# A fused four-block network on one core: the fourth group's expert choice placed directly behind the third's in the first router, ahead of the second half of the second pair's projections

## The chip, the cores and the metric

The kernel runs on one core of one Trainium2 chip. The metric is device time in microseconds (us) of one execution of the whole program. The engines are TensorE (PE), VectorE (DVE), ScalarE (ACT), GpSimd (POOL) and SyncE (SP); each runs its own program in order, and they meet through semaphores.

## What is computed

Four blocks follow one another on x of shape (4, 1024, 256), each one normalised at its entry and added back: a gated recurrence, a mixture of 8 experts with two chosen for each token, causal attention with 16 heads, and a mixture of 32 experts with four chosen. The change lies where the first block ends and the router of the second begins:

```python
x = x + _L0_attn_ref(_layernorm(x), ...)        # ends with einsum('bsn,dn->bsd', h_seq, Wp) + bp
x = x + _L0_ffn_ref(_layernorm(x), w12, w3, gate_w)
# _L0_ffn_ref:
scores = jnp.einsum('btd,ed->bte', x, gate_w)
topk_scores, topk_idx = jax.lax.top_k(scores, 2)
topk_probs = jax.nn.softmax(topk_scores, axis=-1)
hidden = jax.nn.silu(h1) * h2                    # h12 = x @ w12 of the expert
y = jnp.sum(total_probs[..., None] * expert_out, axis=-2)
```

## The kernel before

The 4096 tokens are 32 tiles of 128 rows, kept in SBUF as `X`. The recurrence runs over two pairs of batches (p = 0 and 1), 16 tiles each, since one pair fills the 128 partitions with 2 times 64 states. Its last step is `projections(p, tiles)` on PE (one matmul for each tile) and `add_projections(p, tiles)` on DVE (the sum into `X`, and `bn_stats` of the tile before it); `pair_moments(p)` makes mean and inverse deviation of all 16 tiles of the pair.

The first router works on NG = 8 groups of 4 tiles, g = 0 to 7. Groups 0 to 3 (the first to the fourth) belong to the first pair of batches and groups 4 to 7 (the fifth to the eighth) to the second; GP is 4 and QT is 8. For one group the work goes from engine to engine:

- DVE `rows_of(g)`: the normalised rows into one of RBUF = 4 buffers `b_rows`. From group 4 on it needs `pair_moments(1)`.
- PE `router_transposes(g)`: 8 transposes into PSUM banks 6 and 7. ACT `take_xT(g)` copies them out. PE `router_scores(g)`: 16 small matmuls into bank 2 or 3.
- DVE `choose_pair(g)`: the two best of 8 scores, the score gap, the one-hot rows `b_ohs`. ACT `router_exp(g)`: the exponential of the gap. PE `count_before(g)`: how many tokens before each one went to the same expert.
- DVE `place_pair(g)`: gates and the row slots `b_slot`, from the counts. POOL then issues 8 indirect DMAs, which scatter the group's rows into the experts' regions of the DRAM tensor `routed0`.

`low_weights` and `high_weights` split the experts' first matrices in two parts for the tile products. They lie between the groups: ACT makes the high parts, DVE the low parts of the half k = 1 (eight calls) and six of the half k = 0, POOL the last two of k = 0. After group 7 a plan is made from the counts, the ends of the experts' regions are zeroed, and the loop over 71 expert tiles starts when the plan is there, all scatters have landed, and all low parts are ready.

All order on an engine is written out by hand. The scores and counts of group g share bank 2 + g % 2; `router_scores(g)` waits until the prefixes of group g - 2 have been read. SP has the stores of `X` and the zero fills of the accumulators in its own queue beside all this.

Of the kernel before, what the change touches and what calls it, by code (L numbers as in the profile page):

```python
# [45 lines left out]
def network(nc, x_in, a_params, w12T, w3T, gate0T, wqkT, wvT, woT, swT, bias1, ewT, out):  # L46
# [14 lines left out]
    NG = T // GT  # L61
# [6 lines left out]
    QT = S // P  # L68
# [17 lines left out]
    with ExitStack() as ctx:  # L86
# [370 lines left out]
        def tile_of(t, n):  # L457

            return X[:, bass.ds(t + n, 1), :].rearrange("p a d -> p (a d)")
# [145 lines left out]
        GP = 2 * S // GT  # L605
# [395 lines left out]
        def _(act):  # L1001
# [46 lines left out]
            def take_xT(g):  # L1048
                act.wait_ge(s_btp, g + 1)
                act.activation(b_xT[g % 2][:, :, :].rearrange("p k t -> p (k t)"),  # L1050
                               PS[:, 6:8, :].rearrange("p a n -> p (a n)"), ACT.Copy).then_inc(s_bxT, 1)

            def router_exp(g):

                act.wait_ge(s_bgap, g + 1)
                act.activation(b_ex[:, :], b_gap[:, :], ACT.Exp).then_inc(s_bex, 1)

            def high_weights(k, half):

                act.wait_ge(s_bw, 16 * E0 * KD)  # L1060
                for e in range(half * E0 // 2, (half + 1) * E0 // 2):
                    cols = slice(e * 2 * H0, (e + 1) * 2 * H0)
                    act.activation(b_w12h[k][:, cols], b_w12T[:, k, cols], ACT.Copy).then_inc(s_wh, 1)
# [29 lines left out]
            scan_exps(1, 2)  # L1093
            take_xT(1)
            for g in range(1, NG):
                if g + 1 < NG:
                    take_xT(g + 1)
                router_exp(g)
                if g in (GP - 1, GP):
                    high_weights(1, g + 1 - GP)  # L1100
                if g == NG - 2:

                    act.wait_ge(s_bxn, NT)
                    act.wait_ge(s_xs, 16 * (NG + 1))
                if g >= NG - 2:
                    high_weights(0, g + 2 - NG)
# [369 lines left out]
        def _(dve):  # L1476
# [62 lines left out]
            def add_projections(p, tiles):  # L1539

                for n in tiles:
                    dve.wait_ge(s_abp, p * (2 * QT) + (n + 1))
                    dve.wait_ge(s_ay, p * (2 * QT) + (n + 1))
                    dve.tensor_tensor(tile_of(p * (2 * QT), n), PS[:, 4 + n % 2, 0:D], tile_of(p * (2 * QT), n),
                                      ALU.add).then_inc(s_x1, 1)

                    if n:
                        dve.wait_ge(s_x1, p * (2 * QT) + n)
                        st.done(dve.bn_stats(a_stat[:, n - 1, :], tile_of(p * (2 * QT), n - 1)))
# [14 lines left out]
            def rows_of(g):  # L1564

                if g >= RBUF:
                    dve.wait_ge(s_bxnf, g - RBUF + 1)
                apply_norm(dve, g * G, b_rows[g % RBUF][:, :, 0:D], s_bxn)
# [31 lines left out]
            def place_pair(g):  # L1600

                n = g % RBUF
                st.done(dve.tensor_reduce(b_gsum[:, :], b_ohs[:, :, :].rearrange("p g e -> p e g"), AX_X, ALU.add))

                dve.wait_ge(s_bex, g + 1)
                st.done(dve.tensor_scalar(b_den[:, :], b_ex[:, :], 1.0, None, ALU.add))
                st.sync()
                st.done(dve.reciprocal(b_den[:, :], b_den[:, :]))
                st.sync()
                st.done(dve.tensor_tensor(b_rows[n][:, :, SECOND], b_den[:, :], b_ex[:, :], ALU.mult))  # L1610
                st.sync()
                st.done(dve.tensor_tensor(b_rows[n][:, :, GAP], b_den[:, :], b_rows[n][:, :, SECOND], ALU.subtract))
                dve.wait_ge(s_bpre, g + 1)
                pre = PS[:, 2 + g % 2, 256:256 + G * E0].rearrange("p (g e) -> p g e", g=G)
                for k in range(K0):
                    st.done(dve.tensor_tensor(b_tmp[:, :, k, :], b_oh[:, :, k, :], pre, ALU.mult))
                st.sync()
                dve.sem_inc(s_bpr, 1)
                st.done(dve.tensor_tensor(b_sum[:, :], b_sum[:, :], b_gsum[:, :], ALU.add))
                st.done(dve.tensor_reduce(b_pos[:, :, :].rearrange("p g k -> p (g k)"),  # L1620
                                          b_tmp[:, :, :, :].rearrange("p g k e -> p (g k) e"), AX_X, ALU.add))
                st.sync()
                st.done(dve.scalar_tensor_tensor(b_slot[n][:, :, :], idx, float(REGION), b_pos[:, :, :], ALU.mult, ALU.add))
                st.sync()
                dve.sem_inc(s_bslot, 1)
# [20 lines left out]
            add_projections(1, range(QT))  # L1646
            choose_pair(2)
            place_pair(2)
            add_projections(1, range(QT, 2 * QT))
            pair_moments(1)  # L1650
            rows_of(4)
            for g in range(GP - 1, NG):
                choose_pair(g)
                if g >= GP:
                    low_weights(1, 2 * (g - GP) + 1)
                place_pair(g)
                if g < NG - 1:
                    low_weights(1, 2 * (g + 1 - GP))
                if g + 2 < NG:
                    rows_of(g + 2)  # L1660
# [466 lines left out]
            for n in range(2):  # L2127
                g = NG - 2 + n
# [75 lines left out]
        def _(pe):  # L2204
# [28 lines left out]
            def projections(p, tiles):  # L2233

                pe.wait_ge(s_ah, p + 1)
                for n in tiles:
                    b, t = n // QT, n % QT
                    if n >= 2 or p:

                        pe.wait_ge(s_x1, p * (2 * QT) + (n - 1))  # L2240
                    else:
                        pe.wait_ge(s_axT, GP * KD)
                    pe.matmul(PS[:, 4 + n % 2, 0:D], a_h[p][:, t * P:(t + 1) * P], a_wpT[b], start=True, stop=True).then_inc(s_ay, 1)
# [21 lines left out]
            def count_before(g):  # L2265

                pe.wait_ge(s_boh, g + 1)
                for q in range(G):
                    dst = PS[:, 2 + g % 2, 256 + q * E0:256 + (q + 1) * E0]
                    pe.matmul(dst, onesb[:, :], b_sum[:, :], start=True, stop=False)  # L2270
                    for r in range(q):
                        pe.matmul(dst, onesb[:, :], b_ohs[:, r, :], start=False, stop=False)
                    ins = pe.matmul(dst, tri[:, :], b_ohs[:, q, :], start=False, stop=True)
                ins.then_inc(s_bpre, 1)
# [16 lines left out]
            router_transposes(1)  # L2291
            router_scores(1)
            for g in range(1, NG):
                if g + 1 < NG:
                    router_transposes(g + 1)
                count_before(g)
                if g + 1 < NG:
                    router_scores(g + 1)
                if g <= 2:
                    projections(1, range((g - 1) * QT, g * QT))  # L2300
            pe.wait_ge(s_boh, NG + 1)
            pe.matmul(PS[:, 0, 0:E0], onesb[:, :], b_sum[:, :], start=True, stop=True).then_inc(s_bpre, 1)
            pe.wait_ge(s_bplan, 2)
# [605 lines left out]
```

## Time and profile before

| | |
|---|---|
| median of 3 runs | 2199.08 us (2198.98 to 2201.33) |
| the profiled execution, its own time | 2198.34 us |
| its span in the profile | 2196.1 us |
| mean granted PE clock | 0.935 of full speed |

The profile is of one execution. Times in it are microseconds from the start of the span. A row of a timeline has the start, the length, the engine, the line, the operation and the tiles out<-in; the number in square brackets is the idle time of that engine before the row, and what ended it. "remote" is a release that the profile can't put down to an instruction, and "issue" is time in which it shows no wait. Line numbers are those of the code above.

### The profile page before, as it was taken

How to read it: one execution, taken by the hardware profiler on the slowest of the kernel's cores; microseconds unless marked ns; L12 is line 12 of the kernel's file. 1: busy time of each engine (PE TensorE's matmuls, PEld its weight loads, DVE VectorE, ACT ScalarE, POOL GpSimd, SP SyncE). 2: the span in 40 equal slices, each digit the busy share in tenths (PEclk: the TensorE clock that was granted, in tenths of full speed). 3: DMA queues.
4: the chain of work that ended last, by engine and by line, in shares of the span. 5: the costliest groups of instructions: out<-in, count | busy, mean ns of one | idle time of the engine just before them, and what ended most of it. 6: DMA issues, size and time to landing. Idle time of an engine off the chain costs nothing. (4 is left out here: it accounts for less than half of the span.)

```text
span 2196.1 us, 42575 instructions
## 1 busy us (share of the span) xinstructions
PE 1923.5 (88%) x11815; PEld 1444.0 (66%) x11816; DVE 1361.8 (62%) x3638; ACT 1079.2 (49%) x2250; POOL 1175.1 (54%) x1159
## 2 busy tenths in 40 slices
PE   4852999999689999999999999999999999974870
PEld 2541788888567677677777677777677777752660
DVE  6765343443367777656777656777656877653763
ACT  5321334333355555646655546555646565521760
POOL 3455233232216665536587735577845677835782
PEclk8765999999889999999999999999999999986995
DMA  9652533333331211211121101121101121121979
GB/s 337 213 204 83 125 51 51 51 51 53 79 91 50 56 51 48 54 32 53 50 75 44 48 24 53 50 57 48 45 28 52 47 59 46 39 94 53 205 132 255
DMA packets 215710, 177.59 MB, mean 81 GB/s; under 512 B 85442, under 2 KB 200727, under 8 KB 214880
## 3 DMA queue, kind: packets, MB, share of 16 engines
q1 hardware_dynamic: 177904, 138.78, 21.5%
q0 software_dynamic: 28656, 27.61, 8.3%
q10 hardware_dynamic: 8960, 8.92, 1.2%
q8 instruction: 88, 1.44, 0.3%
q14 instruction: 102, 0.84, 0.1%
HBM read 95.05 MB, written 80.72 MB: 80 GB/s over the span
## 5 line engine op out<-in xcount | busy, mean ns | idle before, releaser
L950 POOL TENSOR_TENSOR c_den_late<-c_den_late,c_p 128x512 f32<-128x512 f32 (+3 forms) x384 | 408.9, 1065 | 247.6 <-ACT c_p L1259 203.6
L1259 ACT ACTIVATE c_p<-PS 128x512 f32<-128x512 f32 (+3 forms) x768 | 342.9, 491 | 230.1 <-PE PS L2470 128.6
L2491 PE MATMUL PS<-c_p,c_vh 128*64 128x256 f32 (+1 forms) x2816 | 322.0, 349 | 0.0
L2439 PE MATMUL PS<-c_k,c_q 128*128 128x512 f32 (+2 forms) x768 | 288.2, 376 | 16.3 <-DVE c_max L1828 5.2
L2462 PE MATMUL PS<-c_q,c_k 128*128 128x512 f32 (+2 forms) x768 | 287.4, 378 | 4.1 <-issue 1.8
L2491 PEld LDWEIGHTS PS<-c_p,c_vh 128*64 128x64 f32 x2816 | 204.5, 137 | 102.5 <-issue 39.7
L886 POOL DMA_INDIRECT acc<-b_y,b_tok x71 | 110.5, 1557 | 277.6 <-ACT b_y L1129 242.9
L2463 PE MATMUL PS<-c_q,c_k 128*128 128x512 f32 (+2 forms) x768 | 258.9, 348 | 0.0
L1250 ACT ACTIVATE c_q<-PS 64x512 fp32r<-64x512 f32 x256 | 151.3, 591 | 205.3 <-PE PS L2426 178.4
L1835 DVE CUSTOM_DVE_ANT_0 PS<-PS,c_maskq,c_max 128x128 f32<-128x128 f32 (+3 forms) x256 | 143.0, 559 | 126.1 <-PE PS L2439 90.8
L1828 DVE TENSOR_REDUCE c_max<-PS 128x1 f32<-128x512 f32 x256 | 175.0, 684 | 55.1 <-PE PS L2439 52.5
L950 POOL TENSOR_TENSOR c_den<-c_den,c_p 128x384 f32<-128x384 f32 (+2 forms) x192 | 141.3, 736 | 120.1 <-ACT c_p L1259 94.8
L2439 PEld LDWEIGHTS PS<-c_k,c_q 128*128 128x128 f32 x768 | 145.6, 190 | 89.4 <-DVE c_max L1835 29.2
L1835 DVE CUSTOM_DVE_ANT_0 PS<-PS,c_maskq 128x128 f32<-128x128 f32 (+3 forms) x256 | 125.9, 501 | 113.8 <-PE PS L2439 101.8
L2462 PEld LDWEIGHTS PS<-c_q,c_k 128*128 128x128 f32 x768 | 145.0, 189 | 33.1 <-issue 15.8
L919 POOL DMA_INDIRECT routed<-r_rows,r_slot x128 | 129.3, 1010 | 61.4 <-DVEq L1946 33.6
L1716 DVE SCALAR_TENSOR_TENSOR b_hid<-b_sg,PS 128x512 f32<-128x512 f32 x71 | 48.8, 688 | 177.4 <-issue 129.6
L2463 PEld LDWEIGHTS PS<-c_q,c_k 128*128 128x128 f32 x768 | 145.3, 189 | 8.8
L2347 PE MATMUL PS<-b_w3T,b_hT 128*128 x568 | 134.7, 380 | 2.0 <-ACT b_hT L1120 1.1
L2330 PE MATMUL PS<-b_w12h,b_tT_hi 128*128 x284 | 129.0, 454 | 5.5 <-DVE b_tT_lo L1709 5.5
L2518 PE MATMUL PS<-c_wo,c_yT 128*128 128x256 f32 x512 | 124.6, 387 | 0.0
L990 POOL DMA_INDIRECT acc<-d_y,d_tok x64 | 100.2, 1566 | 40.7 <-ACT d_y L1439 22.6
(304 smaller groups left out, 4008.8 us busy)
## 6 DMA issues: line engine op xcount, KB each, us to landing
c_vh<-c_v SPq DMA_DIRECT2D x64, 256.0 KB
c_rrow<-rden SPq DMA_DIRECT2D x63, 256.0 KB, 3.7
routed<-b_empty SPq DMA_DIRECT2D x32, 289.0 KB, 9.5
d_xe<-routed SPq DMA_DIRECT2D x32, 289.0 KB
b_xt<-routed SPq DMA_DIRECT2D x71, 130.0 KB
b_w12T<-in_w12T_dram SPq DMA_DIRECT2D x16, 512.0 KB, 13.3
d_acc<-acc SPq DMA_DIRECT2D x16, 512.0 KB, 8.7
c_st_hi<-wqk_split SPq DMA_DIRECT2D x48, 128.0 KB
```

The costliest lines, as they stand in the source:

```text
L919: pool.indirect_dma_start(routed1, bass.IndirectOffsetOnAxis(ap=r_slot[n][:, j // K1, j % K1:j % K1 + 1], axis=0), r_rows[n][:, j // K1, : ...
L950: pool.tensor_tensor(den[:, off:], den[:, off:], p, ALU.add).then_inc(s_cPa, 1)
L1250: act.activation(dst, src, ACT.Copy).then_inc(s_cqs, 1)
L1259: act.activation(c_p[:, P_AT[h][m]:P_AT[h][m] + WIDTH[m]], PS[:, ST_BANK[m % STB], skip:skip + WIDTH[m]], ACT.Exp, scale=ATT_SCALE).then_i ...
L1828: dve.tensor_reduce(dst, src, AX_X, ALU.max).then_inc(s_turn[bank], 1)
L1835: dve.tensor_tensor_reduce(src, src, c_maskq[:, 512 - w:512], 1.0, dst if c else BIG, ALU.add, ALU.max, dst).then_inc(s_turn[bank], 1)
L2330: pe.matmul(PS[:, 2 * j + c, :], b_tT[0][:, j, k, :], b_w12h[k][:, cols], start=(k == 0), stop=False)
L2347: ins = pe.matmul(PS[:, 6 + j, 0:D], b_hT[:, j, k, :], b_w3T[:, k, bass.ds(e * D, D)], start=(k == 0), stop=(k == KH - 1))
L2439: pe.matmul(PS[:, 2 + use[0], 0:max(w, 256)], c_q1[h][:, t * P:(t + 1) * P], c_k1[h][:, c * 512:c * 512 + max(w, 256)], start=True, stop=T ...
L2462: pe.matmul(PS[:, bank, 0:n], c_k1[h][:, j * P:(j + 1) * P], c_q1[h][:, q], start=True, stop=False)
L2463: ins = pe.matmul(PS[:, bank, 0:n], c_k2[h][:, j * P:(j + 1) * P], c_q2[h][:, q], start=False, stop=not diagonal)
L2491: ins = pe.matmul(dst, c_vh[h][:, j, :], moving, start=(j == 0), stop=(t0 == 2 + a))
```

## The change

Three programs are reordered; no instruction is added or removed. The choice and the slots of group 3 move on DVE from behind `pair_moments(1)` and `rows_of(4)` to directly behind group 2's; on PE the count of group 3 moves ahead of the second half of the projections and of the transposes of group 4, and the second half of the projections moves behind that count; on ACT the copy of group 4's transposed rows moves behind the exponential of group 3. On DVE `low_weights(1, 0)` and `rows_of(5)`, which stood around group 3's slots, now follow `rows_of(4)` in the other order.

```diff
@@ scalar engine
             for g in range(1, NG):
-                if g + 1 < NG:
+                if g + 1 < NG and g != GP - 1:
                     take_xT(g + 1)
                 router_exp(g)
+                if g == GP - 1:
+                    take_xT(g + 1)
                 if g in (GP - 1, GP):
                     high_weights(1, g + 1 - GP)
@@ vector engine
             add_projections(1, range(QT))
             choose_pair(2)
             place_pair(2)
+            choose_pair(GP - 1)
+            place_pair(GP - 1)
             add_projections(1, range(QT, 2 * QT))
             pair_moments(1)
-            rows_of(4)
-            for g in range(GP - 1, NG):
+            rows_of(GP)
+            rows_of(GP + 1)
+            low_weights(1, 0)
+            for g in range(GP, NG):
                 choose_pair(g)
                 if g >= GP:
                     low_weights(1, 2 * (g - GP) + 1)
@@ tensor engine
             for g in range(1, NG):
+                if g == GP - 1:
+                    count_before(g)
+                    projections(1, range(QT, 2 * QT))
                 if g + 1 < NG:
                     router_transposes(g + 1)
-                count_before(g)
+                if g != GP - 1:
+                    count_before(g)
                 if g + 1 < NG:
                     router_scores(g + 1)
-                if g <= 2:
-                    projections(1, range((g - 1) * QT, g * QT))
+                if g == 1:
+                    projections(1, range(QT))
```

## Rows read from the trace of the kernel before

**Rows 1.** the page: the span, and busy us, share and instructions of each engine

```profile
span 2196.1 us, 42575 instructions
...
PE 1923.5 (88%) x11815; PEld 1444.0 (66%) x11816; DVE 1361.8 (62%) x3638; ACT 1079.2 (49%) x2250; POOL 1175.1 (54%) x1159
```

**Rows 2.** timeline of DVE (start, us, engine, line, operation; idle before in brackets)

```profile
117.62 0.28 DVE L1616 TENSOR_TENSOR b_tmp<-b_oh,PS 128x32 f32<-128x32 f32 x2
...
118.38 0.17 DVE L1623 SCALAR_TENSOR_TENSOR b_slot<-b_idx,b_pos 128x8 uint32<-128x8 f32 x1
121.89 0.42 DVE L1544 TENSOR_TENSOR X<-PS,X 128x256 f32<-128x256 f32 x1 [3.34 <-issue]
...
128.20 0.41 DVE L1554 BATCH_NORM_STATS2 a_stat<-X 128x6 f32<-128x256 f32 x1
```

**Rows 3.** timeline of PE: scores, projections, transposes, counts

```profile
117.16 3.56 PE L2261 MATMUL PS<-b_gwT,b_xT 128*128 128x8 f32 x16
120.57 0.77 PE L2243 MATMUL PS<-a_par,a_li 128*128 128x256 f32 x1
...
134.67 1.97 PE L506 MATMUL PS<-ident,b_rows 128*128 128x128 f32 x8 [7.83 <-DVE b_rows L499]
136.94 0.19 PE L2270 MATMUL PS<-b_sum,onesb 128*128 128x8 bf16 x1 [0.30 <-DVEq L1598]
...
137.75 3.58 PE L2261 MATMUL PS<-b_gwT,b_xT 128*128 128x8 f32 x16 [0.28 <-ACT b_xT L1050]
...
144.92 0.19 PE L2270 MATMUL PS<-b_sum,onesb 128*128 128x8 bf16 x1 [0.43 <-issue]
```

**Rows 4.** timeline of DVE, from the fifth group's norm to its choice

```profile
133.23 1.38 DVE L499 TENSOR_SCALAR b_rows<-X,means,rstds 128x256 f32<-128x256 f32 x4
134.53 0.18 DVE L1576 COPY b_s<-PS 128x32 f32<-128x32 f32 x1
...
141.09 1.38 DVE L499 TENSOR_SCALAR b_rows<-X,means,rstds 128x256 f32<-128x256 f32 x4
142.38 0.18 DVE L1576 COPY b_s<-PS 128x32 f32<-128x32 f32 x1
```

**Rows 5.** timeline of ACT, the first high part of the weights

```profile
137.69 1.05 ACT L1063 ACTIVATE b_w12h<-b_w12T 128x1024 fp32r<-128x1024 f32 x1
```

**Rows 6.** timeline of DVE, its long idle times from 145 to 177

```profile
151.28 0.28 DVE L1616 TENSOR_TENSOR b_tmp<-b_oh,PS 128x32 f32<-128x32 f32 x2 [4.29 <-remote]
...
166.14 0.19 DVE L1576 COPY b_s<-PS 128x32 f32<-128x32 f32 x1 [3.27 <-remote]
...
172.98 0.17 DVE L1606 TENSOR_SCALAR b_den<-b_ex 128x4 f32<-128x4 f32 x1 [2.50 <-issue]
...
176.26 0.29 DVE L1616 TENSOR_TENSOR b_tmp<-b_oh,PS 128x32 f32<-128x32 f32 x2 [2.50 <-remote]
```

**Rows 7.** busy us of each engine by stretch, PE clock, DMA share, GB/s

```profile
145.00:150.00 5.00, 4.03 (x30) 3.85 (x30) 1.88 (x6) 4.42 (x6) 3.76 (x4) 0.50 0.95 312
150.00:155.00 5.00, 0.08 (x1) 0.08 (x2) 3.36 (x11) 0.00 (x0) 2.16 (x2) 0.50 0.09 32
```

**Rows 8.** timeline of POOL, scatters of the groups and the first low part

```profile
127.77 0.97 POOL L867 DMA_INDIRECT routed<-b_rows,b_slot  x1 [0.30 <-issue]
...
152.54 1.88 POOL L867 DMA_INDIRECT routed<-b_rows,b_slot  x1 [2.87 <-DVEq L1625]
...
177.53 1.88 POOL L867 DMA_INDIRECT routed<-b_rows,b_slot  x1 [3.63 <-DVEq L1625]
...
198.56 2.36 POOL L860 TENSOR_TENSOR b_w12l<-b_w12T,b_w12h 128x1024 fp32r<-128x1024 f32 x1
```

**Rows 9.** timeline of DVE, then of PE, before the first tile

```profile
199.65 3.65 DVE L1700 TENSOR_TENSOR b_tt<-b_tt,b_ts 128x71 f32<-128x71 f32 x1 [1.68 <-remote]
...
211.80 0.79 PE L2330 MATMUL PS<-b_w12h,b_tT_hi 128*128 x1 [4.24 <-DVE b_tT_lo L1709]
```

**Rows 10.** timeline of DVE beside the second router's last scatters

```profile
2001.75 0.69 DVE L2117 SCALAR_TENSOR_TENSOR d_sh<-d_sth,PS 128x512 f32<-128x512 f32 x1 [8.50 <-issue]
```

## The prediction

> **What bounds the kernel now.** I read the page first. PE is busy for 1923.5 of 2196.1 us, DVE, ACT and POOL for about half of it [rows 1], so over the whole kernel PE is the bound. The change lies in a stretch of some 95 us in which this isn't so, and only what moves the end of that stretch, the start of the first expert tile on PE at 211.80 us [rows 9], can move the total: the tile loop, the attention and the last block run behind it in the same order with the same work, so a shift of that start should pass through one to one.
>
> Next I read the timelines of this stretch, engine by engine. DVE ends the slots of the third group at 118.55 (118.38 + 0.17) and then idles for 3.34 us until the first sum of the second half of the projections at 121.89 [rows 2], which PE could begin only at 120.57, behind the fourth group's scores (117.16 + 3.56) [rows 3]. The sums and the moments are a chain of DVE and PE. After them DVE normalises the fifth group at 133.23, and between that and the choice of the fifth group's experts at 142.38 it does the fourth group's choice and slots, one low part, and the sixth group's norm [rows 4]. PE was idle for 7.83 us before the fifth group's transposes [rows 3]. Behind 142.38 come four groups of the same pattern, with POOL's scatters behind them.
>
> Third, I looked for what ends the stretch. POOL starts the fifth group's scatters at 152.54 and the seventh's at 177.53, each time after idling for DVE's slots (2.87 and 3.63 us) [rows 8]. So here POOL follows DVE and not the reverse. Its first low part starts at 198.56 [rows 8], and one of the plan's last operations on DVE, from 199.65 on, takes 3.65 us, until POOL is through with its two low parts [rows 9]. The chain that counts is DVE's, from 121.89 by way of 142.38 to the last slots and the plan.
>
> The fourth thing to see is four idle times of DVE between 145 and 177: 4.29, 3.27, 2.50 and 2.50 us [rows 6], together 12.56. The first is a wait for the fifth group's counts. PE began these at 144.92 [rows 3] and they are short, but DVE went on only at 151.28. The release came more than 5 us late. While it was pending the DMA engines had a share of 0.95, and in the next 5 us 0.09 [rows 7]. I call these late releases.
>
> **The change, step by step.** Nothing is added, so all is in when each piece runs.
>
> Step 1, the choice of the fourth group in the old gap. It can start when its scores are there, 120.72. From its start to the first count matmul the same choice took 136.94 - 134.53 = 2.41 us [rows 3, 4], so PE counts from 123.13. The count lasts no longer than 137.75 - 136.94 = 0.81, of which 0.28 is idle time before the scores, so 0.53 [rows 3]: it ends at 123.66, and only then can PE project. Before, it did at 120.57. The projections, sums and moments, and so the fifth group's norm, shift by 123.66 - 120.57 = **+3.09 us**: the first sum from 121.89 to 124.98, the norm from 133.23 to 136.32. DVE's slots of the fourth group cost nothing extra: from the counts on they took 118.55 - 117.62 = 0.93 [rows 2], so they end at 124.59, 0.4 us ahead of that first sum; the cover is thin, and any lateness of the counts adds to the 3.09.
>
> Step 2, the stretch behind the norm. Before, DVE's own work was its length: 142.38 - 133.23 = 9.15 us. With the fourth group gone it has the two norms and one low part, and the chain through the other engines becomes the length: norm until the transposes 134.67 - 133.23 = 1.44, transposes and ACT's copy until the scores 137.75 - 134.67 = 3.08, scores 3.58, together 8.10 us [rows 3, 4]. The choice of the fifth group begins at 136.32 + 8.10 = 144.42 instead of 142.38: **+2.04 us**. DVE's low part waits for ACT's first high part, which takes 1.05 [rows 5] and starts behind the copy; DVE waits for it in the time that PE has the scores, so it costs nothing; with the cover gone it would cost a little over 1 us.
>
> Step 3, POOL. The fourth group's scatters, whose slots came behind the fifth's norm in the old order, now go directly behind the third's last one, which ends at 128.74 (127.77 + 0.97). A group's eight take (177.53 - 152.54 - 3.63) / 2 = 10.7 us [rows 8], so they are through near 139.5, and POOL is free long before the fifth group's slots. It was waiting for those before too, so the earlier scatters by themselves give nothing. They do leave the DMA queues while SP stores `X` and the fifth group's counts are pending.
>
> Step 4, the late release of 4.29 us. In the new order the fifth group's counts begin 144.92 - 142.38 = 2.54 us behind its choice as before, near 147.0; no scatter is in flight, and the stores share the engines with nothing else, so that they should be finished sooner than at 150. Both things that stood beside the late release are gone. No row tells its cause. From both sides: it stays whole (0) or goes whole (-4.29). I take **-4.29**, since the nearest row on the other side, the busy DMA stretch, is the one that changes.
>
> Step 5, the three later idle times, 8.27 us together. They lie beside the last four groups' scatters, whose order isn't changed. Bounds: all gone (-8.27), or one more of the size seen beside the second router's last scatters, 8.50 us [rows 10]. I take 0.
>
> Sum: +2.04 - 4.29 = -2.25 us. DVE's chain and the scatters behind it shift together, and so does the first tile. The profiled execution took 2198.34 us (its span and 2.24 around it), which gives 2196.1; it was 0.74 below the median of the runs, so against the median of 2199.08 the forecast is 2196.8 us.
>
> At the end of the stretch a rule of the Trainium skill can be held against a row. The 3.65 us operation has both inputs in SBUF and ends at 203.30, POOL's two low parts at 198.56 + 2 x 2.36 = 203.28 [rows 8, 9]. SBUF — State Buffer, "Who interferes with whom", says that such a DVE operation contends with a GpSimd one that reads SBUF, and that the shared port pair is held for the whole instruction; the trace agrees. By the row alone I count nothing here, as both engines shift together. By the rule, a DVE that came 1.1 us earlier relative to POOL would get through first.
>
> **The rivals.**
>
> Rival 1, the late release stays. If 151.28 was fixed by the end of SP's stores, which come no earlier, the later counts are absorbed and the sum is 0: 2199.1 us. If it stays as a length, +2.04: 2201.1. For it: SP's stores are a queue of their own, and the share of 0.95 [rows 7] is mostly theirs. Against it: the scatters' share of the bytes is gone.
>
> Rival 2, slower. Third and fourth groups' scatters now run without a gap from just behind the slots of 118.55 to about 139.5, across the whole second half of the projections. DVE waits there for PE eight times, and every release that is late moves the norm. Beside long runs of scatters releases came late by 3.27 [rows 6] and by 8.50 us [rows 10]. At 8.50 the sum is +6.25: 2205.3. It ends beyond 0.2% only if the lateness exceeds 4.4 + 2.25 = 6.65 us. For it: the run is as long as those. Against it: beside the third group's scatters, in the old order, the sums from 121.89 to 128.61 kept their pace [rows 2].
>
> Rival 3, clearly faster. The three later idle times go too, in whole: 2.04 - 12.56 = -10.52, 2188.6 us. For it: no order of work demands them. Against it: the scatters beside them are unchanged.
>
> Rival 4, DVE gets ahead of POOL at the end and saves what the 3.65 us operation waited, at most about 3.4: -5.65, 2193.4 us. For it: only 1.09 us (199.65 - 198.56) of lead are missing. Against it: POOL was waiting for DVE too, so both shift alike. This is the case in which the skill's rule above would show.
>
> **How the numbers follow.** 0.2% of 2199 is 4.4 us; less than that a measurement of this kernel can't tell from no change. Forecast 0.44, rival 1 0.10, rival 2 0.18, rival 3 0.17, rival 4 0.11. Forecast and rival 1 are the same within 0.2%: 0.54. Faster: 0.28. Slower: 0.18. The range takes in the bounds of the late releases on both sides, 2188.6 to 2205.3, rounded to 2189 and 2205; the forecast's own range is 2194 to 2201. What is sure in the sum is small and against the change; what could be large is the releases, in either direction.
>
> **What the profile after would show.** Step 1: the first sum of the second half near 125.0, the fifth group's norm near 136.3. Step 2: its choice near 144.4, with DVE idle before it. Step 3: no gap between the third and fourth groups' scatters, and POOL idle from 139.5 to 150. Step 4: the fifth group's slots no later than 150, or else the idle time before them still ends at 151. Step 5: idle times of about 8 us between 150 and 175, the first tile on PE near 209.5. The prediction is wrong if releases come late among the projections, or if the idle times of the last four groups differ by more than 4 us from 8.27.

## The result and the profile after

| | before | after |
|---|---|---|
| median | 2197.61 us (14 executions, 2194.01 to 2201.33) | 2205.80 us (14 executions, 2201.52 to 2209.92) |
| the profiled execution, its own time | 2198.34 us | 2207.58 us |
| start of the first expert tile on PE | 211.80 us | 221.07 us |

The ratio is 1.0038 with a 95% interval of 1.0030 to 1.0046: the change makes the kernel slower by 8.2 us. The forecast was 2196.8 us, and the range ended at 2205. Between the two profiled executions lie 9.24 us, and the first tile starts 9.27 us later, so the whole loss arises ahead of it, and I read only that stretch.

The page, the span and the busy times: nothing has become more work (before in [rows 1]).

```profile
span 2205.5 us, 42575 instructions
...
PE 1925.8 (87%) x11815; PEld 1445.5 (66%) x11816; DVE 1364.3 (62%) x3638; ACT 1078.5 (49%) x2250; POOL 1175.2 (53%) x1159
```

The timeline of DVE, from the third group's slots to the fifth group's, answers to [rows 2, 4]. L1618 is the read of the counts, L1625 the slots, L1546 the sum of a projection into `X`, L499 the norm, L1578 the start of a choice.

```profile
118.73 0.17 DVE L1625 SCALAR_TENSOR_TENSOR b_slot<-b_idx,b_pos 128x8 uint32<-128x8 f32 x1
...
129.26 0.28 DVE L1618 TENSOR_TENSOR b_tmp<-b_oh,PS 128x32 f32<-128x32 f32 x2 [4.12 <-remote]
...
130.78 0.42 DVE L1546 TENSOR_TENSOR X<-PS,X 128x256 f32<-128x256 f32 x1 [0.59 <-remote]
...
132.23 0.42 DVE L1546 TENSOR_TENSOR X<-PS,X 128x256 f32<-128x256 f32 x1 [0.69 <-remote]
...
133.66 0.42 DVE L1546 TENSOR_TENSOR X<-PS,X 128x256 f32<-128x256 f32 x1 [0.68 <-PE PS L2249]
...
137.94 0.42 DVE L1546 TENSOR_TENSOR X<-PS,X 128x256 f32<-128x256 f32 x1 [2.07 <-PE PS L2249]
...
142.24 0.42 DVE L1546 TENSOR_TENSOR X<-PS,X 128x256 f32<-128x256 f32 x1 [2.09 <-PE PS L2249]
...
148.01 2.67 DVE L499 TENSOR_SCALAR b_rows<-X,means,rstds 128x256 f32<-128x256 f32 x8
...
156.14 0.19 DVE L1578 COPY b_s<-PS 128x32 f32<-128x32 f32 x1 [1.47 <-PE PS L2267]
...
160.54 0.28 DVE L1618 TENSOR_TENSOR b_tmp<-b_oh,PS 128x32 f32<-128x32 f32 x2
...
161.29 0.17 DVE L1625 SCALAR_TENSOR_TENSOR b_slot<-b_idx,b_pos 128x8 uint32<-128x8 f32 x1
```

Two things catch the eye. The read of the fourth group's counts stands behind 4.12 us of idle time, and seven of the eight sums behind some more, up to 2.09. And at 160.54 the read of the fifth group's counts has no idle time at all, where it had 4.29 before [rows 6].

The timeline of PE, counts and projections (before in [rows 3]):

```profile
123.83 0.19 PE L2276 MATMUL PS<-b_sum,onesb 128*128 128x8 bf16 x1 [2.77 <-DVEq L1600]
...
124.22 2.05 PE L2249 MATMUL PS<-a_par,a_li 128*128 128x256 f32 x4
131.26 1.22 PE L2249 MATMUL PS<-a_par,a_li 128*128 128x256 f32 x2 [4.98 <-issue]
...
138.42 1.22 PE L2249 MATMUL PS<-a_par,a_li 128*128 128x256 f32 x2 [1.61 <-issue]
```

PE has done the counts by 124.4, but DVE reads them at 129.26, 4.9 us later. Then PE itself waits for DVE's first sum (130.78) and goes on at 131.26: from here the two engines take turns, and from sum to sum it is mostly 1.45 or 2.85 us (130.78 to 132.23, 139.39 to 142.24), where the kernel before needed 0.65 to 1.2.

The timeline of POOL, the last scatter of the third group, the first and last of the fourth, and the first of the fifth:

```profile
128.13 0.97 POOL L867 DMA_INDIRECT routed<-b_rows,b_slot  x1 [0.30 <-issue]
130.52 0.96 POOL L867 DMA_INDIRECT routed<-b_rows,b_slot  x1 [1.42 <-issue]
...
139.43 0.97 POOL L867 DMA_INDIRECT routed<-b_rows,b_slot  x1 [0.31 <-issue]
161.79 1.88 POOL L867 DMA_INDIRECT routed<-b_rows,b_slot  x1 [21.39 <-DVEq L1627]
```

The sixteen scatters cover 119.2 to 140.4 with a gap of 1.42 us, and all late turns lie within or just behind them. DVE's idle times behind the fifth group (before in [rows 6]), from its timeline:

```profile
175.41 0.19 DVE L1578 COPY b_s<-PS 128x32 f32<-128x32 f32 x1 [3.28 <-remote]
...
183.70 0.17 DVE L1608 TENSOR_SCALAR b_den<-b_ex 128x4 f32<-128x4 f32 x1 [3.74 <-issue]
...
185.54 0.28 DVE L1618 TENSOR_TENSOR b_tmp<-b_oh,PS 128x32 f32<-128x32 f32 x2 [1.06 <-remote]
```

The balance, in starts of DVE's operations:

| stretch | before | after | difference | forecast |
|---|---|---|---|---|
| up to the fifth group's norm | 133.23 | 148.01 | +14.78 | +3.09 |
| norm to the fifth group's choice | 9.15 | 8.13 | -1.02 | -1.05 |
| choice to the fifth group's slots | 9.66 | 5.15 | -4.51 | -4.29 |
| slots to the first tile on PE | 59.76 | 59.78 | +0.02 | 0 |
| sum | | | +9.27 | -2.25 |

Three of the four terms came out within 0.25 us. The whole miss is in the first.

### The profile page after: what moved, and what is told of

It reads as the page before. It is cut to its first block and busy times, and to the rows that moved or that the text cites. A ratio compares the mean times of both kernels' runs of the same rounds, so it can differ in the third digit from the quotient of the medians.

```text
span 2205.5 us, 42575 instructions
## 1 busy us (share of the span) xinstructions
PE 1925.8 (87%) x11815; PEld 1445.5 (66%) x11816; DVE 1364.3 (62%) x3638; ACT 1078.5 (49%) x2250; POOL 1175.2 (53%) x1159
## 5 line engine op out<-in xcount | busy, mean ns | idle before, releaser
L2528 PE MATMUL PS<-c_wo,c_yT 128*128 128x256 f32 x512 | 124.4, 387 | 0.0
```

## Experiments

Kernels that ran together stand in one set, on the same chip and against the same runs of the kernel before. The median of the kernel before differed from set to set: 2193.23, 2178.59, 2179.65, 2180.04 and 2194.89 us in sets 1 to 5. This turned out to be part of the answer.

The theories. A: releases come late while scatters are in flight; the change puts the counts' release and the turns of PE and DVE under two groups' scatters. B: only the wait for the counts costs, because the slots of the fourth group, now ahead of the first sum, hold up everything behind them. C: SP's zero fills, not the scatters, make releases late.

**Set 1, undo or hold one thing at a time.** First the placing of the fourth group behind the norm, as before, with its choice and counts left where the change has them:

```diff
             choose_pair(GP - 1)
-            place_pair(GP - 1)
             add_projections(1, range(QT, 2 * QT))
             pair_moments(1)
             rows_of(GP)
+            place_pair(GP - 1)
```

> The changed kernel, but DVE makes the fourth group's slots (place_pair(3)) only behind the fifth group's norm; its choice stays ahead of the second half of the sums, and the order of PE and ACT is that of the change. In the changed kernel DVE idled 4.12 us for the fourth group's counts ahead of the first sum, and the first sum came at 130.78 us. Theory A (the second half of the projections is slow because the fourth group's scatters run beside it, and DVE waits for counts whose release comes late): here both are gone. The first sum comes near 125, the sums take about 7 us instead of 13.2, the fifth group's norm comes near 137 instead of 148.0, and the total is 6 to 9 us below the changed kernel. Theory B (only the wait for the counts in front of the sums costs): the first sum near 125.5, but the sums as slow as in the change, the norm near 143, 4 to 5 us gained. Theory C (the zero fills that SP issues in this stretch are what makes releases late, whatever POOL does): the sums keep their 13 us and their two idle times of 2 us, under 5 us gained.

Measured: 2200.70 us, ratio 1.0026 (1.0010 to 1.0041). From the timelines of DVE and of PE:

```profile
128.93 0.42 DVE L1546 TENSOR_TENSOR X<-PS,X 128x256 f32<-128x256 f32 x1 [6.59 <-remote]
...
135.20 0.42 DVE L1546 TENSOR_TENSOR X<-PS,X 128x256 f32<-128x256 f32 x1
```

```profile
122.85 2.05 PE L2249 MATMUL PS<-a_par,a_li 128*128 128x256 f32 x4
129.41 2.08 PE L2249 MATMUL PS<-a_par,a_li 128*128 128x256 f32 x4 [4.50 <-issue]
```

B falls: with no slots in the way the first sum is nearly as late, 6.1 us behind the start of its projection, and the sums, once begun, keep their pace; here the fourth group's scatters start only at 143.7. The two losses are separate. None of the three expectations for this kernel came in whole: A had the first sum near 125 and the norm near 137, and they came at 128.93 and 140.32; the third group's scatters (from 118.17) still stood beside the first projections.

Next, the order of the change with the fourth group's scatters held until all sums are done, and then with both groups' held (`g == 2` in place of 3):

```diff
                 pool.wait_ge(s_bslot, g + 1)
+                if g == 3:
+                    pool.wait_ge(s_x1, 2 * GP * G)
+                    pool.sem_inc(s_pass, 1)
```

> The changed kernel, but POOL begins the fourth group's scatters only when all sums of the second pair are made (one more wait on POOL). DVE still makes the slots ahead of the sums. Theory A (scatters in flight make PE's releases late): the 4 us wait for the counts near 125 stays, since the third group's scatters are in flight there, and the first sum comes near 130 again; from then on no scatter is in flight, so the sums take 6 to 7 us instead of 13.2 and the norm comes near 142 instead of 148.0; the total is 4 to 6 us below the changed kernel, if the fourth group's scatters then don't delay the fifth group's counts. Theory C (the zero fills do it): nothing changes up to the norm, total within 2 us of the changed kernel.

> The changed kernel, but POOL begins the third group's scatters only when all sums of the second pair are made, and so the fourth group's behind them. From 118.9 us until the last sum no scatter is in flight; SP's zero fills are. Theory A: the wait for the fourth group's counts is short (under 1 us), the first sum comes near 125 and the last near 131; the fifth group's norm near 137 instead of 148.0. The sixth group's norm then waits for the third group's scatters (they free its buffer), which costs some 10 us behind that, so the total tells little and the place of the norm decides. Theory C (zero fills): the wait for the counts stays near 4 us and the norm stays near 148.

Measured: 2197.74 us, ratio 1.0017 (1.0005 to 1.0030), and 2197.44 us, ratio 1.0020 (1.0009 to 1.0031). From the timeline of DVE with both held:

```profile
118.47 0.17 DVE L1628 SCALAR_TENSOR_TENSOR b_slot<-b_idx,b_pos 128x8 uint32<-128x8 f32 x1
...
125.24 0.42 DVE L1549 TENSOR_TENSOR X<-PS,X 128x256 f32<-128x256 f32 x1 [0.22 <-DVE b_slot L1628]
...
136.37 2.69 DVE L499 TENSOR_SCALAR b_rows<-X,means,rstds 128x256 f32<-128x256 f32 x8
...
153.27 0.17 DVE L1611 TENSOR_SCALAR b_den<-b_ex 128x4 f32<-128x4 f32 x1 [3.70 <-issue]
```

Without scatters in flight the first sum comes at 125.24 and the norm at 136.37; the forecast had 124.98 and 136.32. So the order of work costs what Step 1 said, and the rest is lateness. With only the fourth group's held, DVE still waits 3.73 us for the counts and the norm is at 140.28, but the sums run at their pace. With both held, the scatters then run across the fifth group's choice, where DVE now waits 3.70 us: the lateness has moved, and neither version beats the kernel before. Both profiles are of the fastest execution of their kernel (2192.78 and 2192.53 us, some 5 below the medians), so their places weigh more than their totals.

Last, the change with SP's zero fills behind the stores of `X`:

```diff
+            sp.dma_start(acc0[T:T + P, :], zeros[:, :]).then_inc(s_xs, 16)
+            for g in range(GP, NG):
+                store_x1(g)
             with sp.Fori(0, NT + C1 // P) as r:
                 sp.dma_start(acc[1][...], zeros[:, :]).then_inc(s_dax, 16)
             ...
-            sp.dma_start(acc0[T:T + P, :], zeros[:, :]).then_inc(s_xs, 16)
-            for g in range(GP, NG):
-                store_x1(g)
```

> The changed kernel, but SP issues the 36 zero fills of the second router's accumulators behind the stores of X instead of in front of them, so that from some 100 us until the last sum the DMA engines carry the scatters alone. Theory A (scatters make releases late): the wait for the fourth group's counts and the slow sums stay, the norm stays within 2 us of 148.0 us, total within 3 us of the changed kernel, unless the fills now meet the last groups. Theory C (zero fills make releases late, alone or together with the scatters): the wait for the counts falls under 1 us and the sums take 6 to 7 us, the norm comes near 137, and the total is 6 to 11 us below the changed kernel.

Measured: 2203.01 us, ratio 1.0039 (1.0026 to 1.0052). From the timeline of DVE:

```profile
124.37 0.28 DVE L1618 TENSOR_TENSOR b_tmp<-b_oh,PS 128x32 f32<-128x32 f32 x2 [1.11 <-PE PS L2279]
...
134.35 0.42 DVE L1546 TENSOR_TENSOR X<-PS,X 128x256 f32<-128x256 f32 x1 [2.04 <-PE PS L2249]
```

C holds for the counts (1.11 us of waiting in place of 4.12) and fails for the sums, which stay slow. In this profile fills and scatters together make the first wait; the scatters alone suffice for the second. The norm is 3.9 us earlier than in the change (144.12), but DVE later waits 4.56 us for the sixth group's counts, and the total gains nothing.

**Set 2, the same questions from the side of the kernel before.** The kernel before and the change once more, the kernel before with the fills moved as above, and the change with this edit on POOL:

```diff
+                if g == GP - 2:
+                    pool.wait_ge(s_bslot, GP)
+                    pool.sem_inc(s_pass, 1)
```

> The kernel before, unchanged, profiled a second time, to see how far a late release belongs to the order of the work and not to one execution. If late releases follow from which transfers are in flight when an engine releases another, the sums of the second half again keep their pace (first near 121.9 us, fifth group's norm near 133), and the idle time in front of the fifth group's slots is again 3 to 5 us. If they are chance, these differ by several us. Ratio to the kernel before 1.000.

> The changed kernel, unchanged, profiled a second time on the chip of this job. If the late releases belong to the order of the work: 3.5 to 5 us of idle time for the fourth group's counts near 125, slow sums, the norm between 145 and 150 us, ratio 1.0038 again. If they are chance: a norm anywhere from 136 to 150.

> The kernel before, but with SP's 36 zero fills behind the stores of X. In the changed kernel the same edit took the wait for the fourth group's counts from 4.1 to 1.1 us, left the sums slow, and gave nothing in total (1.0039 against 1.0038). Theory A (long runs of scatters make releases late): the sums were prompt before and stay so, norm near 133; the fifth group's counts still meet the fourth group's scatters, so that idle time stays at 3 us or more; total within 3 us of the kernel before. Theory C (the fills): that idle time falls under 1 us, and the total is 3 to 5 us below the kernel before, unless the fills, which now meet the last four groups, take it back.

> The changed kernel, but POOL begins the third group's scatters only when the fourth group's slots are made, so both groups' 16 scatters run from about 125 to 146 us. Theory A: no scatter is in flight when PE releases the fourth group's counts, so DVE waits for them under 1 us and the first sum comes near 125.2, as where both were held. The sums then run beside the first 7 us of a run of scatters. If releases come late only some 6 to 9 us into a run, the sums take 6 to 8 us and the norm comes at 136 to 139 instead of 148.0, and what comes late is the transposes and scores of the fifth group. If they come late at once, the norm comes at 141 or later. Total between 1.001 and 1.003 of the kernel before.

Measured, against a kernel before of 2178.59 us: 2178.20 (ratio 0.9993, 0.9984 to 1.0003), 2179.40 (1.0006, 0.9994 to 1.0018), 2178.76 (0.9995) and 2182.27 us (1.0011, 0.9998 to 1.0023). The expectations that counted on late releases missed, and the set doesn't answer what I had asked: no release came late in any of its kernels. The change, timeline of DVE and then of POOL:

```profile
115.24 0.17 DVE L1625 SCALAR_TENSOR_TENSOR b_slot<-b_idx,b_pos 128x8 uint32<-128x8 f32 x1
...
121.70 0.42 DVE L1546 TENSOR_TENSOR X<-PS,X 128x256 f32<-128x256 f32 x1 [0.22 <-DVE b_slot L1625]
...
132.17 2.81 DVE L499 TENSOR_SCALAR b_rows<-X,means,rstds 128x256 f32<-128x256 f32 x8
```

```profile
146.09 1.88 POOL L867 DMA_INDIRECT routed<-b_rows,b_slot  x1 [10.26 <-DVEq L1627]
...
190.51 4.64 POOL L860 TENSOR_TENSOR b_w12l<-b_w12T,b_w12h 128x1024 fp32r<-128x1024 f32 x2
```

The norm is 16.93 us behind the third group's slots, against 13.59 in the kernel before: +3.34, where Step 1 had +3.09. The first tile starts only 0.49 us later (197.15 against 196.66), or 1.16 us counted from the third group's slots (81.91 against 80.75), since POOL goes without a gap from 146.09 to its low parts at 190.51 (190.07 before) and is the bound here, not DVE. So without lateness the change costs about 1 us, 0.05%. The kernel before, too, has its first tile 15.1 us earlier here than in the profile that the prediction was made from (196.66 against 211.80), none of which is owed to the code. Its four idle times of [rows 6] are gone too.

**Sets 3 and 4, the same on two more chips.** Kernel before, change, and the two kernels with held scatters; in set 4 without the one that holds the fourth group's alone.

> The kernel before, a third profile, on the chip on which the next three run. Two kinds of chip have shown so far: one on which releases come late (kernel before at 2193 to 2199 us) and one on which none does (2178 us, fifth group's norm at 129.5 us, no idle time of DVE over 1 us up to the plan). On the first kind: norm near 133, first tile on PE near 212. On the second: first tile near 197. Ratio 1.000.

> The changed kernel beside it. On a chip with late releases: ratio 1.003 to 1.005, norm 12 to 15 us behind that of the kernel before. On one without: ratio 1.000 to 1.001, norm 2.7 us behind, first tile 0.5 us behind.

> The changed kernel with the fourth group's scatters held until the last sum, now on the same chip as the change. On a chip with late releases: wait for the counts still 3 to 5 us, sums prompt, norm 6 to 8 us ahead of the change, 3 to 6 us less in total. On one without: norm as in the change, and the total the same or up to 2 us above it, since POOL, which is then the bound, starts later.

> The changed kernel with the third and the fourth group's scatters held until the last sum, on the same chip as the change. On a chip with late releases: no wait for the counts, norm 11 to 12 us ahead of the change and 3 us behind the kernel before; total 3 to 6 us below the change. On one without: norm as in the change, but POOL's scatters of six groups then run without a gap from the last sum near 127 us on, so the first tile comes 4 us later than in the change or more, ratio 1.002 to 1.004.

> The kernel before, on the chip of this job. Norm of the fifth group near 133 us, with idle times of DVE of 2 to 5 us behind it, if releases come late on this chip; near 129.5 us and none if they don't.

> The changed kernel, on the same chip. If releases come late here: ratio 1.003 to 1.005, norm 12 to 15 us behind that of the kernel before. If not: ratio 1.000 to 1.001, norm 3 to 4 us behind.

> The changed kernel with the third and fourth groups' scatters held until the last sum, on the same chip. If releases come late here: norm 3 us behind the kernel before and 9 to 12 us ahead of the change, total 3 to 6 us below the change; that would show on one chip that the scatters in flight are the condition. If not: ratio 1.002, as on the last chip.

Measured: no late releases in either. The kernel before, run again, stands at 1.0003 (0.9991 to 1.0015) and 0.9990 (0.9978 to 1.0003), the change at 1.0002 (0.9991 to 1.0013) and 1.0005 (0.9992 to 1.0018), the fourth group's scatters held at 1.0006 (0.9996 to 1.0016), both groups' held at 1.0018 (1.0007 to 1.0028) and 1.0016 (1.0003 to 1.0029). Where there is nothing to save by holding scatters, holding them only starts POOL later: counted from the third group's slots, with both held in set 3, its low parts begin after 78.20 us instead of 75.24 in the change, and the first tile after 84.77 instead of 82.01.

**Set 5, the three kernels that matter on one chip.**

> The kernel before, on the chip of this job. With late releases on this chip: norm of the fifth group near 133 us, and idle times of DVE of 2 to 5 us behind it. Without: norm near 129.5.

> The changed kernel, on the same chip. With late releases: ratio 1.003 to 1.005, norm 12 to 15 us behind the kernel before. Without: ratio 1.000 to 1.001, norm 3 to 4 us behind.

> The changed kernel with the fourth group's scatters held until the last sum, on the same chip. With late releases: norm 6 to 8 us ahead of the change, total 3 to 6 us less. Without: the same as the change within 0.1%.

Here the lateness was back. Measured: 2196.40 us (ratio 1.0005, 0.9992 to 1.0017), 2204.38 us (four executions; 1.0048, 1.0031 to 1.0065) and 2198.40 us (1.0025, 1.0011 to 1.0039). From the timelines of DVE, the kernel before, then the change, then the change with the fourth group's scatters held:

```profile
134.37 1.38 DVE L499 TENSOR_SCALAR b_rows<-X,means,rstds 128x256 f32<-128x256 f32 x4
...
152.38 0.28 DVE L1616 TENSOR_TENSOR b_tmp<-b_oh,PS 128x32 f32<-128x32 f32 x2 [4.26 <-remote]
```

```profile
130.54 0.29 DVE L1618 TENSOR_TENSOR b_tmp<-b_oh,PS 128x32 f32<-128x32 f32 x2 [4.66 <-remote]
...
148.72 2.67 DVE L499 TENSOR_SCALAR b_rows<-X,means,rstds 128x256 f32<-128x256 f32 x8
```

```profile
129.03 0.28 DVE L1621 TENSOR_TENSOR b_tmp<-b_oh,PS 128x32 f32<-128x32 f32 x2 [4.14 <-remote]
...
142.20 2.69 DVE L499 TENSOR_SCALAR b_rows<-X,means,rstds 128x256 f32<-128x256 f32 x8
```

The late releases stand where they stood in the result's own profiles, with similar lengths (4.26 and 4.29, 4.66 and 4.12). One held scatter group takes 6.5 us off the norm, 5.0 of them behind the third group's slots (28.71 - 23.72 in the table below), and 6.0 us off the median.

All runs with lateness, and one without for each kernel, in one table. The columns count from the start of the third group's slots, so that what came ahead drops out; the last column is the first tile on PE.

| kernel (set) | to the first sum | first sum to last statistics | to the fifth group's norm | first tile |
|---|---|---|---|---|
| before (the result's) | 3.51 | 6.31 | 14.85 | 211.80 |
| before (5) | 3.12 | 5.92 | 14.85 | 213.00 |
| change (the result's) | 12.05 | 12.79 | 29.28 | 221.07 |
| change (5) | 12.07 | 12.19 | 28.71 | 221.52 |
| slots behind the norm (1) | 11.26 | 6.95 | 22.65 | 216.23 |
| fourth held (1) | 11.24 | 6.46 | 22.39 | 211.25 |
| fourth held (5) | 12.08 | 6.95 | 23.72 | 215.36 |
| fills moved (1) | 7.29 | 12.27 | 25.86 | 219.09 |
| both held (1) | 6.77 | 6.44 | 17.90 | 212.77 |
| before (2), none late | 3.08 | 6.06 | 13.59 | 196.66 |
| change (2), none late | 6.46 | 6.03 | 16.93 | 197.15 |

The first column separates the third group's scatters and the fills, the second the fourth group's scatters.

**Is it PE's clock?** PE's granted clock stood at 0.50 (1.2 GHz, the lower of its two levels) through the change's sums, while in the kernel before it rose to 1.00 (2.4 GHz) among them. That doesn't explain the turns. In set 5, with the fourth group's scatters held, PE had the same clock, shown here by stretch (PE, PEld, DVE, ACT, POOL, then clock, DMA share, GB/s), and the sums took 6.95 us instead of 12.19:

```profile
130.00:135.00 5.00, 3.97 (x9) 2.48 (x10) 3.69 (x10) 0.00 (x0) 0.00 (x0) 0.50 0.39 131
```

By this comparison the low clock is worth at most the 1.0 us by which 6.95 exceeds the 5.92 of the kernel before in that set.

**Is it PE that is late?** The releases that DVE misses come from PE, so I had looked at PE. SP answers the question. Its zero fills run in a loop that waits for no other engine, so its timeline shows the pace of a bystander. From SP's timelines, with start, time to the end of the last, and the number of fills; first the change, then the kernel before, then the change of set 2, then the change with both groups' scatters held (set 1):

```profile
116.08 5.95 SPq L637 DMA_DIRECT2D acc<-zeros  x8
...
121.50 20.60 SPq L637 DMA_DIRECT2D acc<-zeros  x10
...
142.10 4.54 SPq L637 DMA_DIRECT2D acc<-zeros  x7
```

```profile
121.65 8.62 SPq L637 DMA_DIRECT2D acc<-zeros  x5
...
130.27 7.69 SPq L637 DMA_DIRECT2D acc<-zeros  x11
```

```profile
119.33 9.62 SPq L637 DMA_DIRECT2D acc<-zeros  x13
```

```profile
116.91 15.82 SPq L637 DMA_DIRECT2D acc<-zeros  x21
```

In set 2, and in set 1 with the scatters held, the fills keep a beat of about 0.77 us (20 steps and the last fill itself in 15.82 us). In the change they lose it at 121.50 and find it again at 142.10, and between them nine steps take 20.60 us, 2.29 each; in the kernel before the same lasts from 121.65 to 130.27. In both it begins 2.3 to 2.8 us behind the first scatter's start (119.23 and 118.88) and ends 1.5 to 1.7 us behind the last one's end (140.40, and 128.74 in [rows 8]). DVE's sums at 133.66, 137.94 and 142.24 even come 0.10 to 0.14 us behind fills of SP at 133.53, 137.84 and 142.10.

By itself a slow row of fills could still be SP's own DMA queue. Two records speak against that. The trace has the instructions of SP's loop that move a register, count or branch: 0.05 us at most in set 2, from 116 to 129, and in the change, from 121.50 to 142.10, nine of 36 took more than 0.6 us, the longest 0.73. And DVE is late to itself. In the kernel before of set 5 the copy at L485 waits only for DVE's own L483, which ended at 130.20; from its timelines of DVE and of SP:

```profile
131.57 0.17 DVE L485 COPY means<-a_mv 128x16 f32<-128x16 f32 x1 [1.37 <-DVE a_mv L483]
```

```profile
131.45 0.00 SPq L637 DMA_DIRECT2D acc<-zeros  x1
```

In set 2 this copy follows with no idle time (126.70). So PE is not the late engine, or not the only one: SP and DVE are late by themselves too while scatters are in flight, and the change has made of it one stretch of 20.6 us with the counts and all eight sums in it. That one cause stands behind all three is likely from this, and not shown. The record of semaphore updates says where the time lies. In the change the counts' release is on record at 129.23, 4.87 us behind the end of the last count matmul (124.36), and DVE acts on it 0.02 us later; in set 2 the same distance is 0.01 us.

It isn't a lack of transfer capacity. Busy time by stretches (PE, PEld, DVE, ACT, POOL, then clock, DMA share, GB/s) of the change, and of the change in set 2:

```profile
130.00:135.00 5.00, 3.30 (x6) 1.50 (x6) 2.44 (x7) 0.00 (x0) 3.57 (x4) 0.50 0.46 160
```

```profile
120.00:130.00 10.00, 6.88 (x26) 3.77 (x22) 8.86 (x47) 0.00 (x0) 7.55 (x9) 0.77 0.82 278
```

The DMA engines were busy for less than half of the time where the releases were late, and moved 160 GB/s against 278 under scatters and fills in the set without lateness. Nor is it the loading of code: from 120 to 144 us of the change the profile has packets of the scatters' queue and of SP's, and none of an instruction queue.

## Why the prediction was wrong

- **Step 1 failed**, as the term of the sum that was mis-sized: +14.78 us measured against +3.09. Its order of work was right: with both groups' scatters held the norm comes at 136.37 (forecast 136.32), and without lateness the shift is +3.34. What it left out is 11.4 us of lateness (29.28 - 17.90 in the table), 5.3 on the way to the first sum and 6.35 among the sums, less 0.25 behind them; the 0.35 us that is left had arisen ahead of the third group's slots. The step said that "any lateness of the counts adds to the 3.09"; it did, and was priced at nothing, and lateness of the sums did not stand in the step at all.
- **Step 2 was right**: 8.13 us from norm to choice (forecast 8.10), with DVE idle for 2.77 and 1.47 us in it.
- **Step 3 was right in its outcome, wrong in a detail**: POOL was idle for 21.39 us before the fifth group's slots, and the earlier scatters gave nothing. There was a gap of 1.42 us between the groups, since the slots were late too. What I noted in passing, that they leave the DMA queues sooner, was the benefit; that they now run beside the sums was the cost.
- **Step 4 was right**: no scatter in flight, no late release at the fifth group's counts; -4.51 us against -4.29. In the kernel before the late release ended 1.60 us behind the last scatter's end (151.28, and 148.71 + 0.97), as SP's fills do, which speaks for the same mechanism as the loss. The stores were out of the way too (a DMA share of 0.02 from 158 to 161), so this step alone doesn't tell the two apart.
- **Step 5 was right**: 8.08 us of idle times against 8.27.
- **Rival 1** fell with Step 4, rivals 3 and 4 with Step 5. Rival 3's argument, that no order of work demands the later idle times, is true all the same: sets 2 to 4 have none of them. Rival 4's argument fell too: DVE's two-input operation now starts 0.37 us ahead of POOL's low parts (207.47 against 207.84) and still takes 5.11 us, to 212.58, just behind their end at 212.48; in set 2, with nothing of POOL's low parts beside it, it takes 0.23. The rule of the Trainium skill, SBUF — State Buffer, "Who interferes with whom", that the two contend, is borne out; my reading that an early DVE gets through first is not, at a lead of 0.37 us.
- **Rival 2 happened**, with the chance of 0.18: its place and its mechanism, at a lateness of 11.4 us in place of 8.50. It had priced one late release. Its row for the size was well read: the operation that idled 8.50 us in [rows 10] has 0.22 at the most in the kernel before of sets 2 and 3. The eight sums are a conversation: two projections fill the two banks, and from there each engine waits for the other, so that lateness can be paid at every turn.

What misled me was the evidence against rival 2, that the sums kept their pace beside the third group's scatters [rows 2]. It is true, and set 5 repeats it. It doesn't carry over to the change, and I can't say why. In the kernel before PE ran its projections in one piece of 6.27 us from 120.57 and the sums started at 121.89, as SP's last fill on the beat; the scatters outlast all eight sums (128.74 against 127.94). In the change counts and sums start when the stretch is under way. Why the sums of before, which lie inside the stretch in which SP's fills are late, were prompt, stays open; so does what the engines share, and why the lateness was there in sets 1 and 5 and in the result, and not in sets 2, 3 and 4. The sets with it had a kernel before of 2193 to 2198 us, the others of 2179 to 2180. It isn't a property of the chip alone: sets 2 and 5 ran on a chip of the same number. Nor is it noise, since in different sets it recurs at the same places with similar lengths.

One thing splits the profiles in the same way. The nine with lateness (the result's two, four in set 1, three in set 5) have 24,218 to 24,385 semaphore updates on record, the eleven without 27,701 to 27,729, at the same number of instructions. So where releases are late, about one record in eight is missing. Whether the recording itself takes part in the lateness, or loses records because of it, no run here tests. Until one does, the 0.38% belongs to the condition in which these executions were recorded, and not to the kernel under every condition.

## What to carry to other kernels

Before moving asynchronous work (here eight indirect DMAs) look at what kind of work runs beside it in its new place: a chain in which two engines take turns can pay a late release at each turn, as it did here. Price such a risk per turn, not once, and let a thin cover (here 0.4 us) count as none. Look for a bystander engine whose loop waits for nobody, and for an engine's waits for itself; together they show whether one engine is late or several are. And compare a reordering of this size on several chips and at several times: here the same change costs 0.38 and 0.48% in some comparisons and 0.02 to 0.06% in others. Count the records of the profiles too before taking them for equals.

## What the runs showed of the hardware

- While indirect DMAs of POOL were in flight, in the profiles with lateness, releases from PE to DVE came microseconds late (4.87 in the change, 7.08 at the most, at the sixth group's counts of the first kernel in set 1), one of DVE to itself left it idle for 1.37 us, and SP's issue of plain DMAs fell from one in 0.77 us to one in 2.29 us on average, at a DMA share of 0.46. The Trainium skill, Perfetto Trace Analysis, "Tensor Engine Instruction (MATMUL, LD_WEIGHTS)", says that the update of the semaphore and its propagation follow behind the end that the profile reports; the trace agrees, at 0.01 us without lateness and 4.87 us with it.
- The same program showed none of this in three of five sets, and its medians were 13 to 19 us lower there (2178.59 to 2180.04 against 2193.23 to 2197.61).
- Taking the scatters away from a stretch restored its times (norm 136.37 against a forecast of 136.32, fills at 0.77 us); moving the fills away shortened the first wait from 4.12 to 1.11 us and left the sums slow.
